# Two attention layers on one core: the set-up in another order on all engines

## The reference

```python
xn = layer_norm(x, norm_w, norm_b)                   # layer 0
q = (xn @ q_w + q_b).reshape(Bx, Tx, H, -1)
k = (xn @ k_w + k_b).reshape(Bx, Tx, H, -1)
att = jnp.einsum('bnhl,bmhl->bnmh', q, k) + (1.0 - mask) * -1000000.0
att = jax.nn.softmax(att, axis=2)
v = ((xn @ v_w + v_b) * src_mask[:, :, None]).reshape(Bx, Tx, H, -1)
y = jnp.einsum('bnmh,bmhl->bnhl', att, v).reshape(Bx, Tx, Dx)
e = jax.nn.silu(emb) @ emb_w + emb_b
scale, shift = jnp.split(e[:, None, :], 2, axis=2)
h = layer_norm(y, sb_norm_w, sb_norm_b) * (1.0 + scale) + shift
x = x + jax.nn.silu(h) @ out_w + out_b
...
q = jax.nn.softmax(q, axis=-1); k = jax.nn.softmax(k, axis=1)   # layer 1
att = jnp.einsum('bnhd,bnhl->bhdl', k, v)
y = jnp.einsum('bnhd,bhdl->bnhl', q, att)
```

## Time and profile before

| | |
|---|---|
| median of 3 runs | 1110.1 us (1108.95 to 1110.1) |
| the profiled execution, its own time | 1106.18 us |
| its span | 1104.4 us |
| PE busy | 1055.1 us, 96% of the span |
| DVE, ACT, POOL busy | 69%, 54%, 41% |
| mean granted clock of PE | 0.989 |

### The profile page before, as it was taken

One profiled execution on the slowest core, in us unless ns is written; L12 is line 12 of the kernel. 1 busy time (PEld: TensorE's weight loads), 2 busy tenths in 40 slices (PEclk: granted clock), 3 DMA queues, 4 the chain that ended last, 5 costly groups with the idle time before them and its releaser, 6 DMA issues. The chain is left out here.

```text
span 1104.4 us, 25954 instructions
## 1 busy us (share of the span) xinstructions
PE 1055.1 (96%) x8696; PEld 910.7 (82%) x8696; DVE 759.8 (69%) x1326; ACT 591.9 (54%) x1960; POOL 449.2 (41%) x783
## 2 busy tenths in 40 slices
PE   4899999999999999999999999999999999999995
PEld 3678888888888888888887778888888888888884
DVE  4556666766667666676568777777777777777764
ACT  4264677766777667776597544333434434333431
POOL 3232343343433434334333444444444444444432
PEclk9998999999999999999999999999999999999997
DMA  7743102111021110111102201111111111111111
GB/s 211 231 168 118 61 25 62 62 40 59 24 62 62 40 59 24 62 62 41 61 25 97 82 28 46 58 59 57 57 57 57 57 57 57 47 47 35 41 39 57
DMA packets 46017, 71.65 MB, mean 65 GB/s; under 512 B 10256, under 2 KB 14448, under 8 KB 45968
## 3 DMA queue, kind: packets, MB, share of 16 engines
q1 hardware_dynamic: 45968, 71.02, 20.1%
HBM read 54.19 MB, written 16.79 MB: 64 GB/s over the span
## 5 line engine op out<-in xcount | busy, mean ns | idle before, releaser
L1267 PE MATMUL bank<-xt_hi,w_hi 128*128 128x256 f32 x768 | 227.9, 297 | 0.5 <-DVE w_lo L828 0.5
L449 POOL TENSOR_SCALAR stat<-stat 128x1 f32<-128x1 f32 x128 | 34.5, 270 | 454.5 <-DVE stat L877 428.2
L1268 PE MATMUL bank<-xt_lo,w_hi 128*128 128x256 f32 x768 | 218.2, 284 | 0.0
L1269 PE MATMUL bank<-xt_hi,w_lo 128*128 128x256 f32 x768 | 218.0, 284 | 0.0
L607 ACT ACTIVATE prob<-prob,neg_max 128x128 f32<-128x128 f32 x512 | 198.5, 395 | 5.9 <-DVE neg_max L900 5.9
L626 ACT ACTIVATE th<-z_s 128x512 f32<-128x512 f32 x64 | 40.5, 632 | 249.5 <-POOL z_s L483 249.4
L1267 PE MATMUL bank<-w_hi,xt_hi 128*128 128x512 f32 x384 | 157.9, 411 | 1.0 <-DVE w_lo L828 1.0
L1267 PEld LDWEIGHTS bank<-xt_hi,w_hi 128*128 128x128 f32 x768 | 148.7, 194 | 5.5 <-DVE w_lo L828 2.0
L1269 PE MATMUL bank<-w_hi,xt_lo 128*128 128x512 f32 x384 | 150.5, 392 | 0.0
L1268 PE MATMUL bank<-w_lo,xt_hi 128*128 128x512 f32 x384 | 149.8, 390 | 0.0
L1268 PEld LDWEIGHTS bank<-xt_lo,w_hi 128*128 128x128 f32 x768 | 148.2, 193 | 0.0
(11 more groups left out here) (130 smaller groups left out, 2205.7 us busy)
## 6 DMA issues: line engine op xcount, KB each, us to landing
x_in<-in_x_dram SPq DMA_DIRECT2D x32, 256.0 KB, 2.8
x_res<-in_x_dram SPq DMA_DIRECT2D x32, 256.0 KB, 2.9
between_layers<-x_res SPq DMA_DIRECT2D x32, 256.0 KB, 2.0
x_in<-between_layers SPq DMA_DIRECT2D x32, 256.0 KB, 2.8
x_res<-between_layers SPq DMA_DIRECT2D x32, 256.0 KB, 2.7
out_dram<-x_res SPq DMA_DIRECT2D x32, 256.0 KB, 2.5
room<-in_L_cond_W_emb_dram SPq DMA_DIRECT2D x8, 512.0 KB, 5.7
prob<-in_L_cond_emb_w_dram SPq DMA_DIRECT2D x4, 512.0 KB, 7.8
```

The lines of the kernel that those rows point to most:

```text
L449: pool.tensor_scalar(v[:, 8:9], v[:, 7:8], EPS, None, ALU.add).then_inc(s[a_in].sem, 1)
L1267: pe.matmul(o, a_hi, b_hi, start=start, stop=False)
L1268: pe.matmul(o, a_hi, b_lo, start=False, stop=False)
L1269: return pe.matmul(o, a_lo, b_hi, start=False, stop=stop)
```

## The change

Set-up and step 0 are put in another order on every engine; later steps and all sizes stay. On SP, x goes ahead of the norm's parameters and waits for nothing; WQ and WK come next, WV's bias, QB, WV, cond; x of pair 1, the masks and the rest follow, WO now ahead of the embedding's weight; the load of the mask's rows for pair 0 goes ahead of layer 1's parameters; in step 0 the second residual and the first four slices of layer 1's embedding go ahead of the load of the mask's row. On POOL the memset of `mask_wide` goes behind the norms of pair 0 and gets its own semaphore `wide_clear`, so that `consts` is signalled by the instruction before it. On ACT and DVE the split of WQ comes ahead of that of x, whose two halves stand between and behind the halves of WQ. On PE the mask's transposes and `bias_part` of WK move behind the first products of the queries, the transposes of cond ahead of the values, the turns of pair 1 ahead of `embed`; in step 0 `film` moves behind the first half of the queries and the first four slices of layer 1's `embed` ahead of the turns of the last two groups of probabilities.

```diff
@@ sync
-                    sp.wait_ge(*done(s["xn_full"], n + (b - 2)))
-                    sp.wait_ge(*done(s["stats"], n + (b - 2)))
+                    if n.reg is not None or n.const >= GROUP:
+                        sp.wait_ge(*done(s["xn_full"], n + (b - 2)))
+                        sp.wait_ge(*done(s["stats"], n + (b - 2)))
...
             def start():
+                load_front(0, pair(0))
                 load_norm(0)
-                load_front(0, pair(0))
                 load_weight(0, WQ)
+                load_weight(0, WK)
+                load_wide(0, WV, VALUE_BIAS[0])
+                load_col(0, QB, WQ, par_in[0])
+                load_weight(0, WV)
+                sp.dma_start(cond_rows, t["cond_2048"]).then_inc(cond_in, 16)
+                load_front(0, pair(1))
...
+                load_weight(0, WO)
                 load_emb(0, range(4))
-                load_front(0, pair(1))
-                load_weight(0, WO)
...
                 sp.dma_start(mask_bias, mask_tmp[0][:, P:2 * P]).then_inc(mask_saved, 16)
+                for b in range(GROUP):
+                    load_mask(pair(0), b)
                 load_norm(1)
...
             def step0(i, n, f, k, late, slot):
                 load_front(1 if i == G - 2 else 0, n)
                 load_back(0, k, 0)
+                if i == 0:
+                    load_back(0, k, 1)
+                    sp.wait_ge(emb_pe, KE)
+                    load_emb(1, range(4))
                 load_mask(f, 0)
@@ gpsimd
-            pool.tensor_tensor(pick[:], ident[:, 0:2 * B], ident[:, 2 * B:4 * B], ALU.add).then_inc(once, 1)
-            pool.wait_ge(once, 7)
-            pool.memset(mask_wide[:], 0.0).then_inc(consts, 1)
+            pool.tensor_tensor(pick[:], ident[:, 0:2 * B], ident[:, 2 * B:4 * B], ALU.add).then_inc(consts, 1)
...
                 for b in range(GROUP):
                     norm1(pair(0), b)
+                pool.memset(mask_wide[:], 0.0).then_inc(wide_clear, 1)
@@ scalar
-                for b in range(GROUP):
-                    xt_high(f, 0, b)
-                high_part(0, WQ)
+                high_part(0, WQ, (0, 1))
+                xt_high(f, 0, 0)
+                high_part(0, WQ, (2, 3))
+                xt_high(f, 0, 1)
...
@@ vector
+                for b in range(GROUP):
+                    stats1(f, b)
                 spread_norm_b(0)
...
+                low_part(0, WQ, (0, 1))
+                xt_low(f, 0, 0)
+                low_part(0, WQ, (2, 3))
+                xt_low(f, 0, 1)
...
                 for b in range(GROUP):
                     xt_low(pair(1), 1, b)
+                embed_sum(0, 0, 5)
...
+                if i == 0:
+                    embed_sum(1, 0, 6)
                 softmax(k, 1, (3,))
@@ tensor
+                bias_part(0, WQ, 2)
+                need(0, WQ)
+                queries0(f, 0, 0)
+                bias_sum(0, WQ, 5, True)
+                bias_part(0, WK, 3)
+                queries0(f, 0, 1)
                 claim(4, times(mask_ready, 1))
...
                 for b in range(GROUP):
                     turn(pair(1), b)
+                embed(0, range(KE), 5, EMB_SUMS[0])
...
                 scores(k, 1 - slot, 0)
+                queries0(f, slot, 0)
                 if i == 0:
                     film(0, 5)
-                queries0(f, slot, 0)
                 queries0(f, slot, 1)
                 turn_probs(k, 0, (0, 1))
                 scores(k, 1 - slot, 1)
...
+                if i == 0:
+                    embed(1, range(4), 6, EMB_SUMS[1])
                 turn_probs(k, 0, (2, 3))
                 keys(0, f, slot, 0)
-                if i == 0:
-                    embed(1, range(4), 6, EMB_SUMS[1])
```

More of the change, by code:

```diff
@@ L363, in start @@
                                  mask_parts[:, j, :]).then_inc(mask_moved, 16)
-                for b in range(GROUP):
-                    load_mask(pair(0), b)
                 sp.wait_ge(bias_sum_pe, 3)
@@ L374, in step0 @@
                     store(0, late, 1)
-                load_back(0, k, 1)
-                if i == 0:
-                    sp.wait_ge(emb_pe, KE)
-                    load_emb(1, range(4))
+                if i != 0:
+                    load_back(0, k, 1)
                 load_mask(f, 1)
@@ L658, in start @@
                 f = pair(0)
-                for b in range(GROUP):
-                    xt_high(f, 0, b)
-                high_part(0, WQ)
+                high_part(0, WQ, (0, 1))
+                xt_high(f, 0, 0)
+                high_part(0, WQ, (2, 3))
+                xt_high(f, 0, 1)
                 bias_part_out(0, WQ, 2)
                 high_part(0, WK)
+                act.wait_ge(bias_dve, 1)
+                q_out(f, 0, 0)
                 bias_part_out(0, WK, 3)
                 high_part(0, WV)
-                act.wait_ge(bias_dve, 1)
-                q_out(f, 0, 0)
+                act.wait_ge(cond_in, 16)
+                act.activation(tanh_rows, cond_rows, ACT.Tanh, scale=0.5).then_inc(cond_act, 1)
                 q_out(f, 0, 1)
@@ L670, in start @@
                 high_part(0, WO)
-                act.wait_ge(cond_in, 16)
-                act.activation(tanh_rows, cond_rows, ACT.Tanh, scale=0.5).then_inc(cond_act, 1)
                 act.wait_ge(bias_dve, 2)
@@ L1005, in start @@
             def start():
+                f = pair(0)
+                for b in range(GROUP):
+                    stats1(f, b)
                 spread_norm_b(0)
[L1007 to L1014 removed]
+                low_part(0, WQ, (0, 1))
+                xt_low(f, 0, 0)
+                low_part(0, WQ, (2, 3))
+                xt_low(f, 0, 1)
                 low_part(0, WK)
                 bias_col(0, WQ, QB, 5)
+                cut_mask(0)
                 low_part(0, WV)
[L1018 removed]
                 for b in range(GROUP):
                     stats1(pair(1), b)
[L1021 to L1022 removed]
                 dve.wait_ge(cond_act, 1)
@@ L1025, in start @@
                                          op0=ALU.add, op1=ALU.mult).then_inc(cond_dve, 1)
-                bias_wide(0, WV, VALUE_BIAS[0], 5)
-                dve.wait_ge(bias_dve, TURN[0, WV])
-                v_add(0, FIRST, pair(0), 0, 0)
+                bias_col(0, WK, KB, 5)
+                dve.wait_ge(mask_pe, 1)
+                dve.tensor_copy(mask_col[:], bank[4][:, 0:2 * B]).then_inc(mask_ready, 1)
+                low_part(0, WO)
                 dve.wait_ge(cond_pe, 1)
@@ L1031, in start @@
                                   ).then_inc(cond_dve, 1)
-                v_add(0, FIRST, pair(0), 0, 1)
-                embed_sum(0, 0, 5)
+                bias_wide(0, WV, VALUE_BIAS[0], 5)
+                dve.wait_ge(bias_dve, TURN[0, WV])
+                v_add(0, FIRST, f, 0, 0)
+                cut_mask(1)
+                v_add(0, FIRST, f, 0, 1)
                 for b in range(GROUP):
                     xt_low(pair(1), 1, b)
+                embed_sum(0, 0, 5)
             def step0(i, n, f, k, late, slot):
@@ L1431, in start @@
                 keys(0, f, 0, 1)
-                need(0, WV)
-                values(0, FIRST, f, 0, 0)
-                bias_sum(0, WV, 5, False)
                 claim(2, times(cond_dve, 2))
@@ L1439, in start @@
                 last.then_inc(cond_pe, 1)
+                need(0, WV)
+                values(0, FIRST, f, 0, 0)
+                bias_sum(0, WV, 5, False)
                 values(0, FIRST, f, 0, 1)
-                embed(0, range(KE), 5, EMB_SUMS[0])
                 for b in range(GROUP):
                     turn(pair(1), b)
+                embed(0, range(KE), 5, EMB_SUMS[0])
             def step0(i, n, f, k, late, slot):
                 scores(k, 1 - slot, 0)
+                queries0(f, slot, 0)
                 if i == 0:
                     film(0, 5)
-                queries0(f, slot, 0)
                 queries0(f, slot, 1)
```

31 lines of the change are left out of this document (5 added, 26 removed).

## The result

The changed kernel takes 1097.8 us (median of 5 runs, 1095.7 to 1098.1). The kernel before, timed beside it, takes 1110.1 (5 runs, 1107.1 to 1110.3). The ratio is 0.989, with an interval of 0.987 to 0.991. The profiled execution of after took 1097.78 us by its own time (span 1096.0), that of before 1106.18: the two traces differ by 8.4 us, the medians by 12.3. Both numbers have to be explained.

A forecast was written before the change was run, and what follows sets the result against it. PE bounds the kernel, so only set-up and step 0 can gain. Terms -6.2 + 2.2 + 1.2 - 2.0 - 2.2 - 1.5 - 1.7 + 0.4 = -9.8 us, from 1110.1 to 1100.3; range 1096.1 to 1105.1.

The forecast's parts named there:

- First product: Set-up: with x and WQ loaded earlier, the first product of the queries begins at 13.7 instead of 19.9 us, -6.2.
- Clock at the start: First queries: PE runs at the 1.2 GHz level for 5 us after 13.7, +2.2 (0 to +2.6).
- Bias part of WK and the masks' transposes: Between the queries' halves and likewise: work that lay under the wait enters PE's path, +1.0 and about +0.2.
- hole of cond: Ahead of cond's transposes: PE's idle time goes, as cond's silu now precedes WO and the transposes precede the values, -2.0.
- hole of the scores: Ahead of the first scores: PE's idle time goes, as the turns of pair 1 precede `embed`, -2.2.
- No fall behind the first scores: Step 0: without the hole and with `film` behind the first queries, the clock stays up, -1.5 (0 if it falls).
- Layer 1's `embed`: Step 0: its first four slices go under PE's waits for ACT's exponentials, -1.7 (-0.7 at the low end).
- rival D: Slower, over 1112.3: SP's wait for the `mask_bias` write delays layer 1's embedding slices; chance 0.05.
- ACT's +0.4: Step 0: the weighing and the turns behind it come close to ACT's copies and exponentials, +0.4 (0 to 1.5).
- Second fall of the clock: End of step 0: the fall behind the 1.59 us hole ahead of step 1's scores stays, no gain counted.
- rival B: The clock is kinder, with fewer or shorter falls: 13 us gained, 1097; chance 0.12.
- Rival A: Some comes back: several terms at their low end, WQ late +0.8; 5 us gained, 1105; chance 0.23.

The follow-up runs named there:

- experiment 5: Changed kernel with the turns of pair 1 behind `embed` again, and DVE's low parts of pair 1 behind the embedding's sum; 1101.7 us, one execution.
- experiment 6: Changed kernel with layer 0's `film` right behind the first scores again, ahead of the first half of the queries; 1098.0 us in one execution.
- Experiment 7: Changed kernel with the first four slices of layer 1's `embed` behind the keys again; 1096.5 us in one execution.
- Experiment 8: Changed kernel with SP's load of the second mask row behind the last four slices of layer 1's embedding; 1093.5 us in one execution.
- 9: Changed kernel with layer 1's `film` ahead of step 0's output on PE and ahead of the residual's sum on DVE; 1095.5 us in one execution.
- experiment 11: Changed kernel once more without an edit, beside the kernel before; 1096.7 us (4 runs), ratio to before 0.988.
- experiment 4: Changed kernel with 31 unread matmuls in PE's empty time ahead of the first product; 1093.9 us (4 runs), ratio to before 0.985.
- experiment 1: Kernel before with only the early load of x and the memset behind the norms; 1104.9 us (10 runs), ratio to before 0.9954.
- 2: Changed kernel with x split ahead of WQ again on ACT and DVE; 1096.5 us in one execution.
- 3: Changed kernel with one unread activation ahead of everything, so ACT loads its table early; 1094.0 us in one execution.
- 12: Changed kernel with early table, x halves ahead of WQ halves, 16 unread matmuls, layer 1's `film` earlier, slices ahead of the mask row; 1090.0 us (5 runs), ratio to before 0.982.
- Experiment 10: Kernel before, profiled once more without an edit; 1108.3 us in this execution.

## Why the prediction was right, and where its terms were off

The value, 1100.3, was 2.5 us above the result, and the sum of -9.8 stands against -8.4 in the first pair of traces, 11.8 in the second and 12.3 between the medians. Most terms held; that the sum came so near was partly luck, since two misses and a kinder clock cancelled. Term by term, by the first pair:

- **First product, -6.2 (-5.4 to -6.9): -4.9, outside its own range.** The chain was right, but WQ landed at 8.89 and not 7.8, and from there it took 6.1 us instead of 5.9. The parts took 4.9 and 5.6 us to land, the slower one as in the earlier trace rows; I should not have taken the median, since ACT's wait is for both parts (it starts when the second is there), and less data ahead in the queue didn't help. By the Trainium skill's "DMA: Bandwidth & Descriptors", section "Anatomy of one DMA", 512 KB would take an estimated 3.2 us; that figure is for DMAs which the general engine issues, and these are SP's. The trace of after speaks against it here as that of before did. Behind an empty queue it comes nearer: of four parts of 512 KB issued from 84.66 on, the quickest landed after 3.7 us and the slowest after 7.6. By my own words I am wrong if the first product comes after 15; it came at 15.02, and in six other executions with the same order up to there (5 to 9 and 11) at 15.16 to 15.89, since WQ landed later still. This term is the first that failed.
- **Clock at the start, +2.2: measured 2.2**, in experiment 4. The matmuls of the first half are 0.21 us apart while the column of the granted clock says 1.00 (the row of 14 to 16 above). The pace, not the column, decided: in the trace of after the first entry for the clock is a rise at 20.0 us, just where the pace changes, and ahead of its first entry the column says 1.00. Where there is an earlier entry the two agree, as in experiment 11:

```profile
16.00:18.00 2.00, 2.00 (x11) 2.00 (x11) 2.00 (x4) 1.14 (x2) 0.00 (x0) 0.50 1.11 277
```

The 2.2 is the upper end. The first half took 5.15 us in after and 5.2 in experiment 5, but 4.3 to 4.7 in 6 to 9 and 11, against 2.95 at full pace.
- **Bias part of WK and the masks' transposes +1.2, hole of cond -2.0, hole of the scores -2.2.** First scores less first product is 29.81 us in after and 30.75 in before. The terms give 2.2 + 1.2 - 2.0 - 2.2 = -0.8, measured -0.9. Experiment 5 brings the 2.2 of the scores back alone. No experiment isolates the hole of cond; experiment 1, without its remedy, had 1.22 there instead of 2.04.
- **No fall behind the first scores, -1.5: -1.6**, and 1.55 in experiment 5. In experiment 6, without the hole, no fall came; `film`'s place alone was worth 0.6. One execution each can't show that the hole was needed.
- **Layer 1's `embed`, -1.7: -1.74, but 1.3 given back.** Experiment 7 shows both. I had followed the first four slices through SP's queue (rival D) and not the last four: these stood behind a wait for DVE's last reading of the mask's row, and now they were wanted 9 us earlier. Experiment 8 took this away. My condition "wrong if PE waits over 1 us for a DMA" was met by the three waits together, 2.1 us, not by any one of them. The step that failed is the missing term; its place is one line of SP's list. ACT's +0.4 didn't appear.
- **Second fall of the clock, kept in the forecast: -1.2.** It was shorter. This is rival B at half its size. The hole ahead of it stayed as I had said, 1.59.
- Behind step 2 another 0.6 us is lost, none of it in the steps of layer 0: the gain is 9.0 still at step 13, 8.8 late in layer 1 and 8.4 at the end. I left this aside, and its cause is open.

So -4.9 + 2.2 + 1.2 - 2.0 - 2.2 - 1.6 - 1.7 + 1.3 - 1.2 = -8.9, read -9.0 at step 2 and -8.4 at the end. Two misses, 1.3 each and of one sign, were partly made good by the clock's 1.2, and that was luck: I had kept the second fall. Rival A named the kind of loss (terms at their low end, WQ late) and rival D the mechanism of the second one; D's own size, 10 us, didn't come, as the slices for the first half landed in time. They had little to spare: in experiments 2, 3 and 12, where PE comes there earlier, it waits 1.1 to 2.8 us for them (in 4, as early, it doesn't).

**The other 4 us.** I took the pair's sum over to the medians unchanged. The medians moved 12.3 us and the traces 8.4. Experiment 10 gives a cause for part of it: in before the clock can fall behind each of three holes, and its profiled execution was one of its better ones. The second pair of traces differs by 11.8, and what it has beyond the first pair came up by the first turn of probabilities, where the clock had been lower for longer in before. That the falls make up all 3.9 us is not shown; I have two traces of before, and the second one is still 0.6 below the median of its own runs. The forecast, which took its clock from the first trace alone, missed this part.

## What to carry to other kernels

In these traces a hole of the bounding engine costs its length and, behind it, half pace for some microseconds in some executions and not in others. Whoever closes it can gain more in the median than one profile promises, and here the runs spread less too (2.4 us in 9 runs of after, 7.6 in 28 of before). When work is pulled forward, follow every queue that feeds it to its last load, including the waits of loads that have nothing to do with it: one line of SP's list took back three quarters of what the moved half of `embed` had gained. And an operation that is only there for a unit to be ready (a table, a clock) can be placed in idle time by a dummy; the two of them gave here more than the careful interleaving of ACT's and DVE's work.

## What was not expected of the hardware

- The granted clock is shown as 1.00 in the first 20 us of after while matmuls of 256 columns come every 0.21 us, and 0.12 after that. With products that nothing reads ahead of them they come every 0.12 from the start.
- A hole of 1.6 us ahead of the scores of step 1 was followed by a fall of the clock in after, and by none in experiment 8 with the same hole.
- A steady step (the mean from step 2 to step 13) took 34.27 and 34.29 us in the two kernels with the early table load and the additional tile, and 34.40 to 34.43 in the twelve other traces, with the same work and the clock at 1.00 throughout. The cause is open.
- WQ's later part landed at 8.9 us in after, 9.4 in experiment 11 and 9.6 in experiment 4, with its issue at the same time.
